# A gated graph network on one core: the candidate's product with a goes between the reset and the update gate, the norms' products move to another PSUM tile, and GpSimd's copies wait for the turned state

## The reference

```
h = max(layernorm(x), 0);  x = x + attention(h)      # layer 0
h = max(layernorm(x), 0);  x = x + gated_graph(h)    # layer 1

attention: q, k, v = h Wq', h Wk', h Wv'
           rel = adj' * (q k');  rel = rel / norm of its rows;  result rel v
gated_graph, three steps:
    a = adj h                                  (a_in = a_out = a)
    z = sigmoid([a a] w3' + h u3' + biases)    # update gate
    r = sigmoid([a a] w4' + h u3' + biases)    # reset gate
    c = tanh([a a] w5' + (r*h) u5' + biases)   # candidate
    h = (1 - z) h + z c
```

## Time and profile before

| | |
|---|---|
| time, median of 3 runs | 977.67 us (972.51 to 977.94) |
| the profiled execution's own time | 979.97 us |
| its span, first to last instruction | 977.8 us |
| granted TensorE clock, mean | 0.990 |
| one round of six windows, 439.91 to 557.01 us | 117.10 us |
| its windows k = 2, 3, 4, 5, 0, 1 | 25.19, 17.12, 25.19, 17.19, 16.38, 16.03 us |
| PE busy in that round | 113.91 us |
| DVE, ACT, POOL busy in it | 92.81, 63.76, 14.40 us |

### The profile page before, as it was taken

One profiled execution on the slowest core, in us unless ns is written; L12 is line 12 of the kernel. 1 busy time (PEld: TensorE's weight loads), 2 busy tenths in 40 slices (PEclk: granted clock), 3 DMA queues, 4 the chain that ended last, 5 costly groups with the idle time before them and its releaser, 6 DMA issues. The chain is left out here.

```text
span 977.8 us, 14664 instructions
## 1 busy us (share of the span) xinstructions
PE 932.1 (95%) x4816; PEld 779.2 (80%) x4816; DVE 745.8 (76%) x1484; ACT 518.8 (53%) x893; POOL 112.1 (11%) x161
## 2 busy tenths in 40 slices
PE   7799999999999999999999999999999999999997
PEld 6677888788877878788787888887888788877885
DVE  4857777877688777887778878688778877697655
ACT  4546465465545564465635556356465466545553
POOL 1110010201021010210102101020101201020000
PEclk9899999999999999999999999999999999999999
DMA  5004131532225222351324413144131432223122
GB/s 169 1 21 151 63 110 46 171 129 86 86 86 168 90 86 86 111 173 59 108 92 143 150 43 129 64 150 150 64 107 61 154 129 86 86 86 129 65 65 86
DMA packets 75377, 98.72 MB, mean 101 GB/s; under 512 B 8160, under 2 KB 65760, under 8 KB 75360
## 3 DMA queue, kind: packets, MB, share of 16 engines
q1 hardware_dynamic: 75360, 98.50, 30.0%
HBM read 50.76 MB, written 47.71 MB: 101 GB/s over the span
## 5 line engine op out<-in xcount | busy, mean ns | idle before, releaser
L719 ACT ACTIVATE r_s<-gate,b_r 128x512 f32<-128x512 f32 x96 | 65.7, 689 | 192.7 <-PE gate L377 192.7
L983 DVE TENSOR_TENSOR c_s<-z_s,c_s 128x512 f32<-128x512 f32 x96 | 65.8, 686 | 61.5 <-ACT c_s L738 60.7
L1006 DVE TENSOR_TENSOR rh<-r_s,h 128x512 f32<-128x512 f32 x96 | 63.6, 690 | 47.4 <-ACT r_s L719 47.4
L375 PE MATMUL gate<-h_hi,W_hi_u 128*128 128x512 f32 x192 | 79.9, 416 | 16.1 <-DVE norm L905 16.1
L738 ACT ACTIVATE c_s<-cand,b_c 128x512 f32<-128x512 f32 x96 | 64.4, 687 | 44.6 <-PE cand L377 43.5
L375 PE MATMUL gate<-a_hi,W_hi_wz 128*128 128x512 f32 x192 | 80.4, 419 | 4.9 <-ACT r_s L719 0.2
L375 PE MATMUL gate<-a_hi,W_hi_w 128*128 128x512 f32 x192 | 77.3, 403 | 4.8 <-DVE a_lo L827 4.8
L827 DVE TENSOR_TENSOR h<-c_s,d_s 128x512 f32<-128x512 f32 x96 | 78.8, 821 | 3.3
L324 POOL TENSOR_TENSOR rstd<-vare,minus_half 128x4 f32<-128x4 f32 x32 | 41.1, 1284 | 317.1 <-DVE vare L855 317.1
L375 PE MATMUL cand<-rh_hi,W_hi_u 128*128 128x512 f32 x192 | 76.4, 398 | 0.0
L376 PE MATMUL gate<-h_lo,W_hi_u 128*128 128x512 f32 x192 | 75.8, 395 | 0.0
(11 more groups left out here) (128 smaller groups left out, 2230.4 us busy)
## 6 DMA issues: line engine op xcount, KB each, us to landing
h_back<-h_trip SPq DMA_DIRECT2D x244, 128.0 KB, 2.8
h_trip<-h_turned SPq DMA_DIRECT2D x47, 512.0 KB, 2.7
x_s<-x SPq DMA_DIRECT2D x16, 512.0 KB, 4.5
out<-o_s SPq DMA_DIRECT2D x16, 512.0 KB, 3.0
hx_trip<-hx SPq DMA_DIRECT2D x14, 512.0 KB, 3.0
hx_back<-hx_trip SPq DMA_DIRECT2D x56, 128.0 KB, 2.8
h_trip<-h_blk SPq DMA_DIRECT2D x14, 512.0 KB, 3.1
z_s<-w_t SPq DMA_DIRECT2D x1, 512.0 KB, 4.1
```

What stands on the lines that cost most here:

```text
L375: nc.tensor.matmul(dst, l_hi, r_hi, start=start, stop=False, skip_group_check=True)
L719: nc.scalar.activation(r_s[:, c, :], gate[:, c, :], ACT.Sigmoid, bias=b_r[:, c:c + 1]).then_inc(r_ready, 1)
L983: nc.vector.tensor_tensor(c_s[:, c, :], z_s[:, c, :], c_s[:, c, :], ALU.mult).then_inc(prod_ready, 1)
L1006: nc.vector.tensor_tensor(rh[:, c, :], r_s[:, c, :], h[s][:, c, :], ALU.mult).then_inc(rh_ready, 1)
```

## The change

The order on TensorE becomes reset gate, candidate's product with a, update gate. The norms are written to the front of the second half of `cand` instead of `gate`; TensorE waits for the tanh of the same window (`c_ready`) before it writes them, and `candidate_a`, instead of `reset_gate`, waits until DVE has taken them (`norm_taken`). On ScalarE the update sigmoid goes behind `normalise` in k = 1 and 5, and behind `normalise` and `take_back` in k = 3. GpSimd's `h0_in_order` and the second `keep_resid` get a wait for a count of turned halves: 12i + 8 is reached when both halves of window k = 4's update are turned, 12i + 12 in the following k = 0, 12i + 14 in the following k = 1. The first `keep_resid` goes behind the second `h0_in_order`. `final` of the pair's first group goes from the end of DVE's window k = 5 to window k = 0, behind `update` (in the last pair it stays). The start ahead of the loop keeps its order.

```diff
@@ GpSimd, in the loop
                 inverse_std(1, 2 * i + 2)
+                pool.wait_ge(h_is_turned, 12 * i + 8)
                 h0_in_order(2 * i + 2, 0)
                 inverse_norm(norm_taken, 2 * i + 2)
                 inverse_std(1, 2 * i + 3)
+                pool.wait_ge(h_is_turned, 12 * i + 12)
+                h0_in_order(2 * i + 3, 1)
                 keep_resid(2 * i + 2, 0, 2 * i)
-                h0_in_order(2 * i + 3, 1)
+                pool.wait_ge(h_is_turned, 12 * i + 14)
                 keep_resid(2 * i + 3, 1, 2 * i + 1)
@@ TensorE
             def norms(g, w):
                 pe.wait_ge(sq_ready, g + 1)
-                pe.wait_ge(z_ready, 2 * w + 2)
-                last = norm_products(gate[:, 1, 0:Q])
+                pe.wait_ge(c_ready, 2 * w + 2)
+                last = norm_products(cand[:, 1, 0:Q])
@@ reset_gate
-                    if o == 1 and norm is not None:
-                        pe.wait_ge(norm_taken, norm)
@@ candidate_a
                         pe.wait_ge(c_ready, 2 * w + (o - 1))
+                    if o == 1 and norm is not None:
+                        pe.wait_ge(norm_taken, norm)
                     linear(cand[:, o, :], "w5", o, a_hi[s], a_lo[s], True, False)
@@ TensorE's window
-                reset_gate(w, s, ..., 2 * i + (k - 1) // 2 if attention and k in (3, 5) else None)
+                reset_gate(w, s, ...)
+                candidate_a(w, s, 2 * i + (k - 1) // 2 if attention and k in (3, 5) else None)
                 update_gate(w, s)
-                candidate_a(w, s)
@@ ScalarE's window
-                update_sigmoid(w)
                 if attention and k == 1:
                     normalise(0, 2 * i + 2, 0, in_blocks=True)
                 elif attention and k == 3:
                     normalise(1, 2 * i + 2, 0, in_blocks=True)
                 elif attention and k == 5:
                     normalise(1, 2 * i + 3, 1, in_blocks=True)
-                if k in (1, 2, 3, 4):
+                if k == 3:
                     take_back(w)
+                    update_sigmoid(w)
+                else:
+                    update_sigmoid(w)
+                    if k in (1, 2, 4):
+                        take_back(w)
@@ VectorE, take_norm
-                norms_by_token(gate[:, 1, 0:Q]).then_inc(norm_taken, 1)
+                norms_by_token(cand[:, 1, 0:Q]).then_inc(norm_taken, 1)
@@ VectorE's window, k == 5
                     kept_part(w, s)
-                    final(2 * i, 0, w, i)
+                    if not new:
+                        final(2 * i, 0, w, i)
@@ VectorE's window, k == 0
                 else:
+                    final(2 * i - 2, 0, w - 1, i - 1)
                     dve.wait_ge(h_new_ready, 4 * i + 2)
                     reset_state(w, s)
```

More of the change, by code:

```diff
@@ L498, in transpose_new, with reset_gate @@
                     last.then_inc(tok_full, 1)
-            def reset_gate(w, s, n_a, norm=None):
+            def reset_gate(w, s, n_a):
                 pe.wait_ge(h_hi_ready, 2 * w + 2)
@@ L524, in update_gate, with candidate_a @@
                     linear(gate[:, o, :], "wz", o, a_hi[s], a_lo[s], False, True).then_inc(z_full, 1)
-            def candidate_a(w, s):
+            def candidate_a(w, s, norm=None):
                 if isinstance(w, int) and w == 0:
@@ L555, in window @@
                     pe.wait_ge(h_lo_ready, 8 * i + 2 * (k - 1))
-                reset_gate(w, s, use("adj %d" % (k - 1)) if k > 1 else use_in_round("adj 0" if k else "adj 5", i - 1),
-                           2 * i + (k - 1) // 2 if attention and k in (3, 5) else None)
+                reset_gate(w, s, use("adj %d" % (k - 1)) if k > 1 else use_in_round("adj 0" if k else "adj 5", i - 1))
+                candidate_a(w, s, 2 * i + (k - 1) // 2 if attention and k in (3, 5) else None)
                 update_gate(w, s)
-                candidate_a(w, s)
                 if attention and k == 2:
```

## The result

In the first comparison the changed kernel took 950.72 us (median of 4 runs, 949.41 to 955.47) and the kernel before 976.68 (4 runs, 972.51 to 977.94): a ratio of 0.975, with a 95% interval of 0.9705 to 0.9796, so some 26 us faster. The forecast was 954, with 936 to 966. The profiled execution took 949.41 us, its span is 947.3.

A forecast was written before the change was run, and what follows sets the result against it. TensorE, busy 95%, sets the pace, but gaps count only if a_lo comes earlier: 3.2 us per round, 22.6 in seven, plus 1.4 in the closing windows, 24 in all, giving 954 on the median's scale, range 936 to 966.

The forecast's parts named there:

- The bound: TensorE's queue sets the pace, gaps of some 43 us are the ceiling; a gain needs the next window's a_lo earlier.
- TensorE alone: Rival: the chain in k = 3 and 5 shortens with TensorE, all gaps go, 42 us, giving 936; chance 0.09.
- k = 2 with k = 3: Gain 0.37 in k = 2 from the covered gap, 0.35 into k = 4, where a_lo limits w4.
- k = 4 with k = 5: Gain 0.37 in k = 4, and 1.39 into k = 0 from an earlier update without the residual-copy collision.
- k = 0: Into k = 1: gain 0.5 without, 0.0 with a full residual-copy hit on r*h; 0.3 taken.
- k = 1: Into k = 2: tanh about 0.4 late but inside the slack of 0.8; gain 0.45.
- The closing windows: Five windows after the rounds: gain 0.37 in four, nothing in the last; 1.4 us in all.
- The rule weighed against the change: VectorE and GpSimd lock a shared port pair per instruction, the loser fully blocks; final would be held at each copy.
- The GpSimd rival: In k = 0 copies hold final, residual copy and r*h collide, stall 1.4; 1.1 per round, 962; chance 0.18.
- The slower rival: The late update gate becomes the new state's last input; kept part, update, a_lo, w4 late, giving 988; chance 0.07.
- its mark: Sign of the slower case: DVE waiting on z_s ahead of its kept part by over 0.7, and TensorE after it.

The follow-up runs named there:

- the last experiment: Changed kernel with split_state behind split_rh in k = 3, turn_h0 ahead of the attention in k = 5, final ahead of kept_part in the last window: 942.48 us, ratio 0.9644.
- orders-alone kernel: Changed kernel's TensorE and ScalarE orders and norms in cand, GpSimd's queue and final as before; against the kernel before: 977.01 us, ratio 0.9993.

## Why the prediction was right, and where its terms were off

**The bound.** Right: some 43 us of gaps were on the table, and the seven rounds won 22, because `a_lo` decides in k = 3 and 5. The norms put back in `gate` (16.1 us of waiting back for 3 us of time) and the state's split moved ahead of the attention (r*h 0.56 earlier, the round 0.57 shorter) show it from both sides; the rival TensorE alone, with a round of 111.3, is refuted.

**Term by term.** k = 2 with k = 3: 0.72 forecast, 0.79 measured. k = 4 with k = 5: 1.76 and 1.62. k = 0: 0.3 and 0.36. k = 1: 0.45 and 0.40. The round: 3.2 and 3.17. From w4 of the second window to w4 of the first window without attention the forecast is 22.6 less the one k = 1 ahead of it, 22.15; measured 804.05 - 781.97 = 22.08. The places were as said: no distance over 0.25 between reset gate and w5, nor inside u3 in k = 3 and 5; pauses at u5 of 0.73 and 0.85 where 0.6 was expected; at w4 of k = 4 0.56; at w4 of k = 0 0.09 in all, where the longer u5 pause ahead of it had taken up the chain's lateness.

**The closing windows were mis-sized: 1.4 forecast, 0.92 measured.** The four between w4 starts fell from 63.28 (895.33 to 958.61) to 61.71 (865.75 to 927.46): 1.57. The last one lost 0.65, from 19.19 to 19.84, where the text counted nothing. Its reason was that the later gate lies ahead of `final` and the last state, which is the cost, not a cover: with no next window there is no work to hide it. VectorE and TensorE at the end of after:

```profile
937.15 1.29 DVE L975 TENSOR_TENSOR o_s<-h_back,resid 128x512 f32<-128x512 f32 x2
938.35 0.69 DVE L989 TENSOR_TENSOR c_s<-z_s,c_s 128x512 f32<-128x512 f32 x1
```

```profile
941.15 1.97 PE L484 MATMUL tok<-ident,h 128*128 128x128 f32 x8 [2.65 <-DVE h L833]
```

In the last experiment `final` stands in VectorE's wait ahead of `kept_part` instead, and from the last w4 to the end it is 19.10.

**Window k = 0 came out right by a detail that was wrong.** The text had the residual copy start first and hold r*h by 0.85. In the trace r*h starts first (511.48), the copy waits and takes 1.52, and it is then the split of r*h behind it that takes 1.96. The sum of the lateness is similar, since the second of both parts waits either way; that the term fitted (0.36 for 0.3) is in this part luck.

**The rule weighed against the change** holds where it was doubted. The forecast took the four small copies at 1.88 as nearly free, but undisturbed they take 1.43 (row in the last section): they had lost 0.45 already in before. Where one operation meets one, the second is held for most of what is left of the first (1.54 for 0.69, 1.52 for 1.03, 1.51 for 1.01). The Trainium skill's page SBUF — State Buffer, section SBUF: two separate sides, says that whichever of the two starts first has the shared port pair for its whole instruction, and the other fully blocks; these rows agree. But the loser was seldom on the path: `final` held by 0.3 and the copies by 0.9 cost little after the move. The GpSimd rival (a round of 115.0) is the round of the kernel without GpSimd's waits, by another collision: the waits do what they are placed for, which that rival denied.

**The slower rival** did not come, though its mark, VectorE waiting for `z_s` ahead of `kept_part` by more than 0.7 and TensorE after it, was met. In k = 5 that wait is 0.86 (the row of the kernel with `final` at the end of k = 5, the same in after), and at w4 behind it 0.09 are lost. In k = 3 of after it is 2.62, and TensorE pauses 0.56 at w4 behind it:

```profile
461.67 1.29 DVE L984 SCALAR_TENSOR_TENSOR d_s<-z_s,h 128x512 f32<-128x512 f32 x2 [2.62 <-ACT z_s L734]
```

But in k = 3 of before VectorE stood 2.57 for the tanh in its place, and the forecast's own working had the sigmoid last there. The mark measured a wait and not a lateness, and was badly chosen. The margin in k = 5 was thin, and the orders-alone kernel shows what happens beyond it.

**The time.** Forecast 954 against 950.7. From w4 of the second window on, the forecast gain was 0.6 too large (22.15 + 1.4 = 23.6 against 23.0). So the 3.3 us by which the kernel is faster than forecast, and these 0.6, are not in the steps of the sum. They go with the granted clock of the runs: at equal clock the gain is about 24, which is what the sum says. The profile of before had lost some 7 us ahead of the second window against that of after. That the medians differ by more than the sum is not the change's doing, as far as the runs show. Why a start falls into one case or the other stays open. No experiment tried it.

## What to carry to other kernels

Before a pause is counted as a gain, follow the data that the next stage needs and ask who delivers them: here 16.1 us of waiting on an engine busy 95% were worth 3, and 0.56 us of VectorE's chain were worth 0.57 a round. Two parts of a change that each bring little can bring much together when each leaves the other's job on the path, so an edit that delays an input (the late sigmoid) has to be timed together with clearing the path behind it. Where an engine waits in its queue with ready jobs behind it, move the waiting job back; look separately at the last stage, which has nothing behind it to hide a later input.

## What the runs showed of the hardware that was not expected

**The clock can fall after a short pause.** In the orders-alone kernel the granted clock of the 4 us behind the 2.3 us pause was 0.57 to 0.69 in three rounds of seven, and 1.00 in four with the same pause. In those three, eight matmuls of 512 columns followed each other every 0.43 us, the lower level of 1.2 GHz, which cost 1.6 us. After the norms' pause, 1.26 more than the usual distance, no steady round of before showed it. The Trainium skill's page TensorE: Matmul & The Clock Gate, Part 1, calls the number of slow matmuls at a kernel's start variable from run to run; here it varied, eight or none, between rounds of one run. What decides it is not shown.

**Four columns can wait half a microsecond.** GpSimd's power of 128 x 4 took 1.51 instead of 1.01 beside VectorE's splits with two inputs in SBUF, and 1.01 in k = 5 of the kernel where transposes with one input ran beside it. Its small size did not spare it.

**Short operations on both sides hold each other.** The four copies of `h0_in_order` took 1.43 where VectorE ran transposes, as in window k = 4 of after:

```profile
468.01 1.43 POOL L335 COPY h<-h_blk 128x256 f32<-128x256 f32 x4
```

They took 1.88 beside one product of the update and 2.35 beside `final`'s pair, and that pair 1.60 instead of 1.29. Together the two lose 0.92 and 0.31, more than the one subtraction behind the residual copy (0.85), but spread over both engines, so that little of it stands on the path.
